# Expert jobs of 128 tokens instead of 256, with the tokens as the stationary operand

## The chip, the cores and the metric

The kernel runs on one core of one Trainium2 chip. The metric is the device time of one execution in microseconds (us). The kernel before was timed three times: 1541.42, 1542.98 and 1551.13 us, a median of 1542.98 us. One further execution was recorded by the hardware profiler; every row below comes from it.

## The reference, cut to what matters

The program computes one layer over 625 nodes of 768 features: a graph attention block, a linear attention block ("mixer"), and a feed-forward block of a shared expert and eight routed experts. The change touches only the routed experts:

```python
h1 = jnp.einsum('td,eid->tei', x2, w1)      # 768 -> 512, each expert e
h3 = jnp.einsum('td,eid->tei', x2, w3)
h = jax.nn.silu(h1) * h3
y = jnp.einsum('tei,edi,te->td', h, w2, cw) # 512 -> 768, weighted by the gate
z = jax.nn.silu(x2 @ sw1.T) * (x2 @ sw3.T) @ sw2.T   # the shared expert
return (y + z)
```

The gate gives every token two experts, so `cw` has 1250 entries that are not zero. The reference's own gate, evaluated on the drawn inputs, sends 332, 144, 157, 53, 209, 113, 224 and 18 tokens to experts 0 to 7.

## The kernel before, in words

The routed part works only on the pairs of token and expert that exist. On the chip, VectorE counts the tokens of each expert, cuts them into **jobs** of `CAP` = 256 places (`BL` = 2 blocks of 128), and writes a list (`lst`) with the token, the target row and the gate weight of each place. The counts above make 2+1+1+1+1+1+1+1 = 9 jobs. A job loads the three weight matrices of its expert whole, in six pieces of 128x1536 float32 (768 KB each): pieces 0 and 1 are w1, 2 and 3 are w3, 4 and 5 are w2.

Products are taken in a split form: each operand is a high part and a low part in the float32r format, and `mm3` (lines 1375 to 1379) issues high x high, high x low and low x high. So each operand passes twice through other engines: ScalarE casts the high part (`split_hi`, line 794, for weights; `tokens_hi`, line 825; line 844 for the hidden rows), VectorE subtracts it to get the low part (`split_lo`, L1192; `tokens_lo`, L1335; L1351). There is one buffer for the raw pieces and one for the split ones (`we`), so piece q of the next job is loaded when `split_lo` has read piece q of this one, and is split when TensorE has used it.

All engines run the same loop over jobs, each its own `body(g, parity)`: jobs 0 and 1 are written out, jobs 2 to `JOBS_MIN` in a loop, the rest in a loop whose bodies are guarded by `If(count > g)`. The order on each engine is fixed by its program:

- GpSimd: gathers the 128-row blocks of the next job's tokens from HBM (`gather_tokens`, indirect DMA, L595), then scatters the two result blocks of this job to `y_rows` (L617) when VectorE has weighted them. The scatter of a block waits until the one before it has landed. The gather of the job after stands behind these scatters in GpSimd's program.
- TensorE: the w1 products of the job (weights stationary, 256 token columns moving), the w3 products, and between them the transposes of the next job's tokens (L1623); then the down products of the same job (hidden rows stationary, 384 columns of w2 moving). An up matrix is 4x6 groups of three matmuls, so 144 matmuls for both; the down products are 48 matmuls.
- ScalarE and VectorE: the splits, Silu (L842), the product with the w3 half (L1349), and the weighting of the result by the gate (L1360, 128x384).
- SyncE: issues the loads of the weight pieces (L472), each after the wait for its buffer.

When all results have landed, SyncE reads `y_rows` back and VectorE adds them to the output (L1368). The shared expert runs before the jobs. While it runs, VectorE makes the job list (`places`, L1251 to L1296), with one instruction for each multiple of `CAP` below 625 (L1262).

Of the kernel before, what the change touches and what calls it, by code (L numbers as in the profile page):

```python
# [17 lines left out]
ALU = mybir.AluOpType  # L18
# [30 lines left out]
CAP = 256  # L49
# [13 lines left out]
def build(nc, x, src, dst, W1s, b1s, W1d, b1d, attn1, ln1_w, ln1_b, Wos, bos, Wod, bod, attno, lno_w,  # L63
          lno_b, qkv_wT, qk_bcols, v_brow, proj_wT, proj_b, proj_matT, gate_wT, gate_bias, moe_w, out):
    ctx = ExitStack()
    with ctx:
# [12 lines left out]
        def dram(name, shape, dt=F32):  # L79
# [66 lines left out]
        jobs_i = sb("jobs_i", [P, 1], I32)  # L146
# [13 lines left out]
        hid_s, raw4, raw5, y_1 = zone([("hid_s", [128, 2, IC, CAP], F32R), ("raw4", [128, PIECE], F32),  # L160
                                       ("raw5", [128, PIECE], F32), ("y_1", [128, D], F32)])
        sb("zone_d", [128, T * N + 4 * D], F32)
        raw3, xg = zone([("raw3", [128, PIECE], F32), ("xg", [128, BL, D], F32)])
# [18 lines left out]

        atg0, atg1, y_0 = zone([("atg0", [128, 2, KC, CAP], F32R), ("atg1", [128, 2, KC, CAP], F32R), ("y_0", [128, D], F32)])
        atg, y_sb = [atg0, atg1], [y_0, y_1]
# [90 lines left out]
        xg_loaded = [sem(f"xg_loaded{i}") for i in range(BL)]  # L275
# [3 lines left out]
        e_hi, e_lo = sem("e_hi"), sem("e_lo")  # L279
# [27 lines left out]
        def jobs(eng, start, body):  # L307

            start()
            for g in range(2):  # L310
                body(g, g)
            with eng.Fori(1, JOBS_MIN // 2) as m:
                for parity in range(2):
                    body(2 * m + parity, parity)
            eng.wait_ge(jobs_ready, 1)
            count = eng.value_load(jobs_i[0:1, 0:1], min_val=JOBS_MIN, max_val=JOBS)
            with eng.Fori(JOBS_MIN // 2, JOBS // 2) as m:
                for parity in range(2):
                    with eng.If(count > 2 * m + parity):
                        body(2 * m + parity, parity)  # L320

        def tg_psum(b):

            return (ps[:, 4 + 2 * b:6 + 2 * b, :].rearrange("p a b -> p (a b)")[:, 1024 - D:1024]
                    .rearrange("p (k n) -> p k n", k=KC))

# [34 lines left out]
        def _(sp):  # L361
# [122 lines left out]
            for q in range(6):  # L484
# [4 lines left out]
                if q >= 4:  # L489
                    sp.wait_ge(e_lo, q - 3)  # L490
                load_piece(ROUTED, q, q % 4)

            def load_pieces(g, qs):
# [3 lines left out]
                for q in qs:  # L497
                    if not isinstance(g, int):
                        sp.wait_ge(e_lo, 6 * g + q + 1)
                    elif q < 4:  # L500
                        sp.wait_ge(e_lo, (5, 6, 3, 4)[q])
                    load_piece(e, q, q)

# [3 lines left out]
            load_pieces(0, (4, 5))  # L507
            with sp.Fori(1, JOBS_MIN) as g:
                load_pieces(g, range(6))
            count = sp.value_load(jobs_i[0:1, 0:1], min_val=JOBS_MIN, max_val=JOBS)  # L510
            with sp.Fori(JOBS_MIN, JOBS) as g:
                with sp.If(count > g):
                    load_pieces(g, range(6))
            load_pieces(count, range(4))

            sp.wait_ge(landed, 16 * BL * count)
# [12 lines left out]
        def _(pool):  # L529
# [59 lines left out]
            def gather_tokens(g):  # L589
                blocks = slice(BL * g, BL * g + BL) if isinstance(g, int) else bass.ds(BL * g, BL)  # L590
                pool.tensor_copy(gather_i[:, :], lst[:, blocks, 0]).then_inc(gather_i_ready, 1)
                pool.wait_ge(gather_i_ready, g + 1)
                for b in range(BL):
                    pool.sem_inc(pool_turn, 1)
                    pool.indirect_dma_start(  # L595
                        out=xg[:, b, :], out_offset=None, in_=xf_rows,
                        in_offset=bass.IndirectOffsetOnAxis(ap=gather_i[:, b:b + 1], axis=0)).then_inc(xg_loaded[b], 16)
# [6 lines left out]
            def body(g, parity):  # L604
                pool.wait_ge(tg_full, BL * g + BL)
                gather_tokens(g + 1)

                if not first(g):
                    pool.wait_ge(landed, 16 * BL * g)
                pool.tensor_copy(scatter_i[:, :], lst[:, bass.ds(BL * g, BL), 1]).then_inc(scatter_i_ready, 1)  # L610
                pool.wait_ge(scatter_i_ready, g + 1)
                for b in range(BL):
                    pool.wait_ge(down_used, 4 * g + 10 + 2 * b + 2)
                    if b > 0:
# [1134 lines left out]
```

## Time and profile before

| | |
|---|---|
| profiled execution, its own time | 1550.59 us |
| span of its core | 1548.8 us |
| median of the three timed runs | 1542.98 us |
| TensorE busy, share of the span | 1108.7 us, 72% |
| VectorE / ScalarE / GpSimd busy | 60% / 35% / 38% |
| bytes moved by DMA | 270.51 MB, 175 GB/s over the span |
| scatters of result blocks (L617) | 18, so 9 jobs of two blocks |
| weight pieces loaded (768 KB each) | 64: 6 for the shared expert, 54 for nine jobs, 4 for a tenth that isn't run |

The two stages of graph attention take most of the span; the job stage lies between 1250 and 1518 us, and from 1518 us on the kernel only reads results back, adds and stores. An engine's busy time is the sum over its instructions; matmuls are pipelined, so the time from one matmul to the next is read from their starts and not from their durations. Times of rows are microseconds from the start of the span.

### The profile page before, as it was taken

To read this page: it belongs to the slowest core of one execution; us is meant where nothing else is said; L and a number is where in the kernel's file an instruction comes from. 1 tells how busy PE (TensorE), PEld (TensorE's weight loads), DVE (VectorE), ACT (ScalarE), POOL (GpSimd) and SP (SyncE) were. 2 spreads that over 40 slices of the span, in tenths; PEclk is the share of its full clock that TensorE was granted. 3 is DMA by queue.
4 is the path that set the end of the run, shared out by engine and by line. 5 is a ranking of instruction groups with operands and counts; after the bars stand their busy time and mean duration, and the time that the engine had idled before them with its cause. 6 is when DMAs were issued, how large, how long until landed. Compare 5 with 4: busy or idle time off the path is not lost.

```text
span 1548.8 us, 17191 instructions
## 1 busy us (share of the span) xinstructions
PE 1108.7 (72%) x6361; PEld 956.7 (62%) x6361; DVE 932.1 (60%) x1695; ACT 536.9 (35%) x754; POOL 586.0 (38%) x578
## 2 busy tenths in 40 slices
PE   6956555555416657998999996008869999989992
PEld 5943333333316647986787775008549999889981
DVE  6548777777757666525445445453786556556564
ACT  3214333333226556202333443001333234434440
POOL 0037777777720000026777777760000001211210
PEclk9986777777857678996999998557977999999996
DMA  9756676767662231348767768643111356755745
GB/s 342 280 195 195 198 198 196 201 195 201 195 164 65 65 86 62 122 145 275 207 204 216 214 194 260 187 143 91 61 60 52 102 224 216 243 194 187 235 148 169
DMA packets 81361, 270.51 MB, mean 175 GB/s; under 512 B 15619, under 2 KB 37417, under 8 KB 80662
## 3 DMA queue, kind: packets, MB, share of 16 engines
q0 software_dynamic: 35296, 148.26, 32.0%
q1 hardware_dynamic: 42502, 107.11, 22.5%
q10 hardware_dynamic: 3488, 14.16, 2.3%
q8 instruction: 46, 0.75, 0.2%
q14 instruction: 29, 0.23, 0.1%
HBM read 236.29 MB, written 33.19 MB: 174 GB/s over the span
## 4 chain that ended last, share of the span: by engine, by line
POOL 29%; PE 25%; DMA 16%; DVE 15%; issue 12%; ACT 3%; SPq 0%; POOLq 0%; DVEq 0%; ACTq 0%
POOL dense_logits L564 10%; POOL ring_s L553 10%; POOL ring_d L559 8%; PE ps L1377 7%; PE ps L1378 7%; PE ps L1379 7%; DMA ring_d<-table_dst,dst_i 5%; DMA xg<-xf_rows,gather_i 3%; DMA y_rows<-y,scatter_i 3%; DVE mxv L1060 3%; DMA dl_a<-dense_logits 3%; DVE ring_s L973 1%; DVE stats L863 1%; PE ps L1468 1%; DMA y_in<-y_rows 1%
## 5 line engine op out<-in xcount | busy, mean ns | idle before, releaser
L973 DVE TENSOR_TENSOR ring_s<-ring_s,ring_d 128x776 f32<-128x776 f32 (+1 forms) x168 | 162.1, 965 | 268.9 <-DMA ring_d<-table_dst,dst_i 268.8
L553 POOL DMA_INDIRECT ring_s<-table_src,src_i x168 | 169.3, 1008 | 397.3 <-DVE fd_stage L902 336.0
L1433 PE MATMUL ps<-hot_s,hot_d 128*125 128x512 f16 (+1 forms) x840 | 185.9, 388 | 157.6 <-DVE hot_s L980 157.5
L1433 PEld LDWEIGHTS ps<-hot_s,hot_d 128*125 128x125 f16 x840 | 116.6, 180 | 227.0 <-DVE hot_s L980 168.1
L564 POOL DMA_INDIRECT dense_logits<-logits,cell_i x168 | 203.0, 1208 | 51.4 <-issue 50.9
L559 POOL DMA_INDIRECT ring_d<-table_dst,dst_i x168 | 164.3, 978 | 51.2 <-issue 51.2
L674 ACT ACTIVATE hot_d<-iota_h,dst_bias 128x626 f16<-128x626 f16 x84 | 68.5, 816 | 219.7 <-PE ps L1433 219.6
L1377 PE MATMUL ps<-atg,we 128*128 128x256 f32 x432 | 123.5, 286 | 2.2 <-DVE atg L1335 2.2
L1378 PE MATMUL ps<-atg,we 128*128 128x256 f32 x432 | 122.5, 284 | 0.0
L1379 PE MATMUL ps<-atg,we 128*128 128x256 f32 x432 | 122.2, 283 | 0.0
L1377 PE MATMUL ps<-wp,at 128*125 128x384 f32 x300 | 105.6, 352 | 7.0 <-DVE at L886 4.1
L1378 PE MATMUL ps<-wp,at 128*125 128x384 f32 x300 | 104.4, 348 | 0.0
L1379 PE MATMUL ps<-wp,at 128*125 128x384 f32 x300 | 104.3, 348 | 0.0
L1468 PE MATMUL ps<-fs,dpt 125*125 125x96 f32 (+1 forms) x500 | 98.7, 358 | 0.0
L1395 PE MATMUL ps<-ident,b 125*128 125x125 f32 x90 | 19.2, 381 | 108.9 <-DVE b L1038 83.9
L617 POOL DMA_INDIRECT y_rows<-y,scatter_i x18 | 17.7, 982 | 200.3 <-DVE y L1360 160.3
L1192 DVE TENSOR_TENSOR we<-eraw,we 128x1536 fp32r<-128x1536 f32 x35 | 60.5, 1756 | 54.3 <-ACT we L794 54.2
L1468 PEld LDWEIGHTS ps<-fs,dpt 125*125 125x125 f32 x500 | 81.6, 233 | 13.1 <-issue 1.8
L1377 PEld LDWEIGHTS ps<-atg,we 128*128 128x128 f32 x432 | 83.0, 192 | 2.4 <-issue 2.4
L1395 PEld LDWEIGHTS ps<-ident,b 125*128 125x128 f32 x90 | 15.4, 201 | 111.6 <-DVE b L1038 84.0
L1509 PE MATMUL ps<-xt,mix_w 128*128 128x313 f32 (+1 forms) x288 | 81.8, 442 | 2.0 <-issue 1.7
L1378 PEld LDWEIGHTS ps<-atg,we 128*128 128x128 f32 x432 | 82.8, 192 | 0.0
(241 smaller groups left out, 2595.5 us busy)
## 6 DMA issues: line engine op xcount, KB each, us to landing
eraw<-in_moe_w_dram SPq DMA_DIRECT2D x35, 768.0 KB, 6.4
raw<-in_moe_w_dram SPq DMA_DIRECT2D x29, 768.0 KB, 6.1
dense_logits<-neg ACTq DMA_DIRECT2D x1, 12288.0 KB, 40.9
mix_w<-in_qkv_wT_dram SPq DMA_DIRECT2D x18, 384.0 KB, 6.5
dl_a<-dense_logits SPq DMA_DIRECT2D x3, 2187.5 KB
dl_b<-dense_logits SPq DMA_DIRECT2D x2, 2187.5 KB
y_in<-y_rows SPq DMA_DIRECT2D x5, 672.0 KB
ring_s<-table_src,src_i POOLq DMA_INDIRECT x168, 4.1
```

The lines of the kernel that those rows point to most:

```text
L553: pool.indirect_dma_start(out=ring_s[:, j, 0:WL[l]], out_offset=None, in_=table_src[l], in_offset=bass.IndirectOffsetOnAxis(ap=src_i[:, t: ...
L559: pool.indirect_dma_start(out=ring_d[:, j, 0:WL[l]], out_offset=None, in_=table_dst[l], in_offset=bass.IndirectOffsetOnAxis(ap=dst_i[:, t: ...
L564: pool.indirect_dma_start(out=dense_logits[l], out_offset=bass.IndirectOffsetOnAxis(ap=cell_i[:, t:t + 1], axis=0), in_=logits[:, t, 0:HL[ ...
L674: act.activation(hot_d[:, j, :], iota_h[:, :], ACT.Square, scale=0.25, bias=dst_bias[:, t:t + 1]).then_inc(hot_square, 1)
L973: dve.tensor_tensor(ring_s[:, j, 0:WL[l]], ring_s[:, j, 0:WL[l]], ring_d[:, j, 0:WL[l]], ALU.add).then_inc(z_ready[l], 1)
L1192: dve.tensor_tensor(we[:, 2 * m + 1, part], src, we[:, 2 * m, part].bitcast(F32), ALU.subtract).then_inc(e_lo, 1)
L1377: pe.matmul(o, lt(0), r(0), start=start, stop=False)
L1378: pe.matmul(o, lt(0), r(1), start=False, stop=False)
L1379: return pe.matmul(o, lt(1), r(0), start=False, stop=stop)
L1433: last = pe.matmul(ps[0:P, b, o:o + s1 - s0], hot_d[:, j, c * P:(c + 1) * P], hot_s[:, j, s0:s1], start=start and (n <= 5 or n == 9), stop ...
L1468: last = pe.matmul(o, pt[:, m * N + s * P:m * N + (s + 1) * P], fs[:, s, col:col + w], start=s == 0, stop=s == T - 1)
L1509: last = pe.matmul(ps[:, b, 0:c1 - c0], mix_w[:, 1 - m, k, s * 128:(s + 1) * 128], xt_v[:, k, c0:c1], start=k == 0, stop=k == KC - 1)
```

## The change

`CAP` becomes 128 and `BL` 1. A job is one block of tokens, with one gather and one scatter. The counts above make 3+2+2+1+2+1+2+1 = 14 jobs. `JOBS_MIN` becomes 10 (it was 4) and `JOBS` 18 (it was 12).

In the up products the operands trade places: the tokens are stationary and 512 columns of a weight matrix move, so a matrix is 6 groups of three matmuls, 36 matmuls for both, and the result has tokens on the partitions. ScalarE and VectorE make Silu and the product in one instruction each of 128x512 (`hid_rows`). The hidden rows then have to be transposed for the down products: four transposes on TensorE into bank 4 (`transpose_hidden`), and a split of 128x512 on ScalarE and VectorE (`hidden_hi`, `hidden_lo`).

The down products of job g-1 (24 matmuls of 384 columns) are issued in body g, behind the up products of job g and the transposes of the tokens of job g+1; the weighting and the scatter of job g-1 move with them. A new `finish` issues the last job's. SyncE loads pieces 0 to 3 of job g+1 ahead of pieces 4 and 5 of job g. The semaphores of the pieces are parted into those for w1 and w3 and those for w2.

```diff
-CAP = 256
+CAP = 128
...
+            finish(eng.value_load(jobs_i[0:1, 1:2], min_val=JOBS_MIN - 1, max_val=JOBS - 1))
...
+            def load_job(g):
+                load_pieces(g + 1, range(4))
+                load_pieces(g, (4, 5))
```

On GpSimd:

```diff
+            def scatter_rows(g):
+                if not first(g):
+                    pool.wait_ge(landed, 16 * g)
+                pool.tensor_copy(scatter_i[:, :], lst[:, bass.ds(g, 1), 1]).then_inc(scatter_i_ready, 1)
+                pool.wait_ge(scatter_i_ready, g + 1)
+                pool.wait_ge(down_used, 2 * g + 12)
...
+            def body(g):
+                pool.wait_ge(tg_full, g + 1)
                 gather_tokens(g + 1)
                 if not first(g):
...
+                    scatter_rows(g - 1)
```

On ScalarE:

```diff
+            def tokens_hi(g):
+                act.wait_ge(tg_full, g + 1)
+                act.copy(atg[:, 0, :, :], tg_psum()).then_inc(tg_hi, 1)
+
+            def hidden_hi(g):
+                act.wait_ge(ht_full, g + 1)
+                act.wait_ge(down_full, 2 * g + 10)
+                act.copy(hid_t[:, 0, :, :], ps[:, HT_BANK, :].rearrange("p (j n) -> p j n", j=IC)).then_inc(hid_hi, 1)
...
+            def body(g):
+                if not first(g):
+                    hidden_hi(g - 1)
                 act.wait_ge(w1_used, g + 1)
                 split_hi(g + 1, (0, 1))
...
+                act.wait_ge(up_full, g + IC + 1)
+                act.wait_ge(hid_f, g + IC)
+                act.activation(silu[:, 0, 0:INTER], ps[:, 0, :], ACT.Silu).then_inc(silu_done, 1)
+                tokens_hi(g + 1)
                 split_hi(g + 1, (2, 3))
...
+                act.wait_ge(down_full, 2 * g + 10)
+                split_hi(g, (4, 5))
```

On VectorE:

```diff
+            def hidden_lo(g):
+                dve.wait_ge(hid_hi, g + IC + 1)
+                dve.tensor_tensor(hid_t[:, 1, :, :], ps[:, HT_BANK, :].rearrange("p (j n) -> p j n", j=IC),
+                                  hid_t[:, 0, :, :].bitcast(F32), ALU.subtract).then_inc(hid_lo, 1)
+
+            def weighted(g):
+                if not first(g):
+                    dve.wait_ge(landed, 16 * g)
+                w = lst[:, bass.ds(g, 1), 2].bitcast(F32)
+                for h in range(2):
+                    dve.wait_ge(down_full, 2 * g + h + 11)
+                    dve.tensor_scalar(y_sb[:, h * HALF:(h + 1) * HALF], ps[:, DOWN_BANKS[h], 0:HALF], w, None, ALU.mult).then_inc(down_used, 1)
...
+            def body(g):
+                if not first(g):
+                    hidden_lo(g - 1)
+                split_lo(g + 1, (0, 1))
+                dve.wait_ge(silu_done, g + IC + 1)
+                if not first(g):
+                    dve.wait_ge(ht_full, g)
+                dve.tensor_tensor(hid_rows[:, :], silu[:, 0, 0:INTER], ps[:, 1, :], ALU.mult).then_inc(hid_f, 1)
+                tokens_lo(g + 1)
+                split_lo(g + 1, (2, 3))
+                if not first(g):
+                    weighted(g - 1)
                 split_lo(g, (4, 5))
```

On TensorE:

```diff
             def transpose_tokens(g):
...
+                pe.wait_ge(xg_loaded, 16 * g + 16)
+                if not first(g):
+                    pe.wait_ge(tg_lo, g)
+                for k in range(KC):
+                    last = pe.transpose(tg_psum()[:, k, :], xg[:, k * 128:(k + 1) * 128], ident[:, :])
+                last.then_inc(tg_full, 1)
+
+            def up(m):
+                for k in range(KC):
+                    last = mm3(ps[:, m, :], lambda s: atg[:, s, k, :], lambda s: w13[m][s][:, k, :], k == 0, k == KC - 1)
+                return last
+
+            def transpose_hidden(g):
+                pe.wait_ge(hid_f, g + IC + 1)
+                for j in range(IC):
+                    last = pe.transpose(ps[:, HT_BANK, j * 128:(j + 1) * 128], hid_rows[:, j * 128:(j + 1) * 128], ident[:, :])
+                last.then_inc(ht_full, 1)
+
+            def down(g):
+                pe.wait_ge(w2_lo, 2 * g + 4)
+                pe.wait_ge(hid_lo, g + IC + 1)
+                pe.wait_ge(down_used, 2 * g + 10)
+                for h in range(2):
+                    for k in range(IC):
+                        last = mm3(ps[:, DOWN_BANKS[h], 0:HALF], lambda s: hid_t[:, s, k, :],
+                                   lambda s: w2v[s][:, k, h * HALF:(h + 1) * HALF], k == 0, k == IC - 1)
+                    last.then_inc(down_full, 1)
...
+            def body(g):
+                pe.wait_ge(up_lo, 4 * g + 6)
+                pe.wait_ge(tg_lo, g + 1)
+                pe.wait_ge(hid_f, g + IC)
+                up(0).then_inc(w1_used, 1)
+                if not first(g):
+                    transpose_hidden(g - 1)
+                pe.wait_ge(up_lo, 4 * g + 8)
+                up(1).then_inc(up_full, 1)
+                transpose_tokens(g + 1)
+                if not first(g):
+                    down(g - 1)
+
+            def finish(last):
+                transpose_hidden(last)
+                down(last)
```

## Rows read from the trace of the kernel before

**Rows 1.** Windows over the job stage; busy us (instructions) of each engine, granted clock, DMA share, GB/s.

```profile
1250.00:1518.00 268.00, 249.02 (x1848) 245.06 (x1848) 158.94 (x181) 117.43 (x146) 41.74 (x52) 0.98 0.61 209
```

**Rows 2.** DMA queues in the job stage: packets, MB, share of 16 engines' time.

```profile
q1 hardware_dynamic: 7776, 42.47, 46.9%
q0 software_dynamic: 2720, 13.37, 13.8%
```

**Rows 3.** Waits of the job stage: who waited for what, us in total, times, longest.

```profile
PE ps L1623 <- DMA xg<-xf_rows,gather_i: 16.7, 12, 3.8
```

**Rows 4.** Timeline of TensorE and chain of waits: starts of the first and last of a run.

```profile
1253.94 0.28 PE L1379 MATMUL ps<-atg,we 128*128 128x256 f32 x1
...
1262.48 0.28 PE L1379 MATMUL ps<-atg,we 128*128 128x256 f32 x1
...
1454.86 0.17 PE ps L1377
...
1458.84 0.19 PE ps L1379
```

**Rows 5.** Groups of instructions, shapes apart, from 1000 us: busy, mean ns, idle before.

```profile
L1192 DVE TENSOR_TENSOR we<-eraw,we 128x1536 fp32r<-128x1536 f32 x35 | 60.5, 1756 | 54.3 <-ACT we L794 54.2
L794 ACT CAST we<-eraw 128x1536 fp32r<-128x1536 f32 x35 | 50.4, 1476 | 49.4 <-PE ps L1379 49.4
L1360 DVE TENSOR_SCALAR y<-ps,lst 128x384 f32<-128x384 f32 x36 | 19.9, 610 | 6.8 <-PE ps L1379 6.8
L1335 DVE TENSOR_TENSOR atg<-ps,atg 128x768 fp32r<-128x768 f32 x20 | 18.6, 955 | 10.8 <-ACT atg L825 10.8
L825 ACT CAST atg<-ps 128x768 fp32r<-128x768 f32 x20 | 15.3, 798 | 22.0 <-PE ps L1623 22.0
L1349 DVE TENSOR_TENSOR silu<-silu,ps 128x256 f32<-128x256 f32 x36 | 15.0, 417 | 12.7 <-ACT silu L842 12.6
```

**Rows 6.** Chain of waits: the weighting of a block and its scatter.

```profile
1459.73 0.62 DVE y L1360
...
1461.16 4.94 DMA y_rows<-y,scatter_i
```

**Rows 7.** Timeline of GpSimd: a scatter and the next gather.

```profile
1317.32 0.98 POOL L617 DMA_INDIRECT y_rows<-y,scatter_i  x1 [4.39 <-DMA y_rows<-y,scatter_i]
...
1319.32 1.00 POOL L595 DMA_INDIRECT xg<-xf_rows,gather_i  x1 [0.82 <-POOL gather_i L591]
```

**Rows 8.** The tile xg (gathers), then first, longest and last of six on the chain.

```profile
DMA to landing us min/median/max: 3.9/5.7/9.6
...
1290.32 6.07 DMA xg<-xf_rows,gather_i
...
1349.69 8.47 DMA xg<-xf_rows,gather_i
...
1470.22 6.15 DMA xg<-xf_rows,gather_i
```

**Rows 9.** Chain of waits: token transposes and the first up product of job 0.

```profile
1249.90 0.89 PE ps L1623 x6
...
1253.62 0.36 PE ps L1377
```

**Rows 10.** Chain of waits: the last scatter.

```profile
1522.48 3.03 DMA y_rows<-y,scatter_i
```

**Rows 11.** Window in which only weight pieces move; columns as in the first group.

```profile
1262.00:1272.00 10.00, 10.00 (x88) 10.00 (x86) 6.82 (x9) 5.92 (x9) 0.00 (x0) 1.00 1.02 422
```

**Rows 12.** Windows around a gap of TensorE, and over the edge stage; columns as before.

```profile
1386.00:1388.00 2.00, 0.00 (x0) 0.00 (x0) 1.53 (x4) 0.69 (x2) 0.45 (x1) 1.00 0.85 304
1388.90:1392.20 3.30, 3.30 (x17) 3.07 (x16) 1.87 (x3) 1.60 (x2) 0.00 (x0) 0.50 0.76 283
...
296.00:500.00 204.00, 99.12 (x500) 70.62 (x500) 147.44 (x224) 76.01 (x96) 109.67 (x105) 0.71 0.62 170
```

**Rows 13.** One line of VectorE: the count of jobs.

```profile
L1262 DVE SCALAR_TENSOR_TENSOR job_count<-before,job_count x2: 168/168/169, 1204.1 to 1204.3; 125x8 f32<-125x8 f32 x2
```

More of the change, by code:

```diff
@@ L274, in build @@
         gather_i_ready, scatter_i_ready = sem("gather_i_ready"), sem("scatter_i_ready")
[L275 removed]
+        xg_loaded, ht_full = sem("xg_loaded"), sem("ht_full")
         tg_full, tg_hi, tg_lo, w1_used = sem("tg_full"), sem("tg_hi"), sem("tg_lo"), sem("w1_used")
@@ L497, in load_pieces @@
                 for q in qs:
[L498 to L501, printed above, removed]
+                    if q >= 4:
+                        if not first(g):
+                            sp.wait_ge(w2_lo, 2 * g + q - 3)
+                    elif not first(g):
+                        sp.wait_ge(up_lo, 4 * g + q + 1)
+                    elif q < 2:
+                        sp.wait_ge(w2_lo, q + 1)
+                    else:
+                        sp.wait_ge(up_lo, q + 1)
                     load_piece(e, q, q)
+            def load_job(g):
+                load_pieces(g + 1, range(4))
+                load_pieces(g, (4, 5))
             sp.wait_ge(jobs_ready, 1)
@@ L512, in _ @@
                 with sp.If(count > g):
-                    load_pieces(g, range(6))
-            load_pieces(count, range(4))
-            sp.wait_ge(landed, 16 * BL * count)
+                    load_job(g)
+            sp.wait_ge(landed, 16 * count)
             for t in range(T):
@@ L602, in start @@
                 gather_tokens(0)
-            def body(g, parity):
-                pool.wait_ge(tg_full, BL * g + BL)
+            def body(g):
+                pool.wait_ge(tg_full, g + 1)
                 gather_tokens(g + 1)
                 if not first(g):
[L609 to L614, printed above, removed]
-                        pool.wait_ge(landed, 16 * BL * g + 16 * b)
-                    pool.sem_inc(pool_turn, 1)
-                    pool.indirect_dma_start(
-                        out=y_rows, out_offset=bass.IndirectOffsetOnAxis(ap=scatter_i[:, b:b + 1], axis=0),
-                        in_=y_sb[b][:, :], in_offset=None).then_inc(landed, 16)
-            jobs(pool, start, body)
+                    scatter_rows(g - 1)
+            def finish(last):
+                scatter_rows(last)
+            jobs(pool, start, body, finish)
         @block.scalar
@@ L1352, in body @@
                 split_lo(g + 1, (2, 3))
                 if not first(g):
-                    dve.wait_ge(landed, 16 * BL * g)
-                for u in range(4):
-                    b, h = u // 2, u % 2
-                    w = lst[:, bass.ds(BL * g + b, 1), 2].bitcast(F32)
-                    dve.wait_ge(down_full, 4 * g + 10 + u + 1)
-                    dve.tensor_scalar(y_sb[b][:, h * HALF:(h + 1) * HALF], ps[:, 4 + u, 0:HALF], w, None, ALU.mult).then_inc(down_used, 1)
-            jobs(dve, start, body)
+                    weighted(g - 1)
@@ L1365, in _, with finish @@
+                split_lo(g, (4, 5))
+            def finish(last):
+                hidden_lo(last)
+                weighted(last)
+            jobs(dve, start, body, finish)
             for t in range(T):
@@ L1619, in transpose_tokens @@
             def transpose_tokens(g):
-                for b in range(BL):
-                    pe.wait_ge(xg_loaded[b], 16 * g + 16)
-                    for k in range(KC):
-                        last = pe.transpose(tg_psum(b)[:, k, :], xg[:, b, k * 128:(k + 1) * 128], ident[:, :])
-                    last.then_inc(tg_full, 1)
+                pe.wait_ge(xg_loaded, 16 * g + 16)
[22 more added lines that the diff above has]
+                    last.then_inc(down_full, 1)
             def start():
```

137 lines of the change are left out of this document (46 added, 91 removed).

## The prediction

> **What bounds the kernel now.** I read the windows first, to find the stage that the change touches: 1250 to 1518 us, 268 us for nine jobs, 29.8 us a job. TensorE is busy 93% of it at a granted clock of 0.98, and the DMA engines 61% [rows 1]. The waits show what ends its idle time: 12 waits for gathered tokens, 16.7 us, where the longest is 3.8 us [rows 3]. So TensorE bounds the stage, with a gather late in most jobs. A busy sum does not price its work; starts do. The 72 steps between the two up matmuls of the timeline take 8.54 us, 0.1186 us for 256 columns, and the 23 steps between the two down matmuls 3.98 us, 0.173 us for 384 [rows 4]. A job before is then 144 x 0.1186 + 48 x 0.173 + 12 transposes (2 x 0.89 [rows 9]) = 17.1 + 8.3 + 1.8 = 27.2 us.
>
> **TensorE after.** 128 columns more cost 0.173 - 0.1186 = 0.055 us, so 512 columns cost 0.228 us; the bounds are 0.213 (512 columns at 2.4 GHz) and 0.237 (twice the 256). Up: 36 x 0.228 = 8.2 us. Down: 24 x 0.173 = 4.15 us. Six token and four hidden transposes at 0.89/6: 1.5 us at most, 1.3 in a stream. Sum 13.7 us (13.1 to 14.1), half of before. But there are 14 jobs instead of 9, and what a job costs the other engines does not halve, since every job splits and loads its expert whole.
>
> **VectorE** after, a job: six subtractions at 1.72 us (a pair takes 3.43, a lone one 1.756 [rows 5]) 10.3; tokens 0.955; weighting two halves 1.1 to 1.2; two new 128x512 instructions, between 0.417 (128x256) and 0.955 (128x768) [rows 5], on the line between them 0.68, so 1.4. Sum 13.8 us. **ScalarE**: 6 x 1.43 to 1.476 + 0.80 + 2 x 0.60 = 10.7 us. It hides beside VectorE.
>
> **DMA.** A job loads 6 x 786 KB = 4.72 MB, as before, and moves one gather and one scatter of 0.393 MB. With only weights moving the engines gave 422 GB/s at a share of 1.02 [rows 11]: 11.2 us for 4.72 MB. Over the whole stage their packets took 46.9% of 268 us for nine sets, 14.0 us a set, and 13.8% for 34 indirect transfers (13.37 MB / 0.393), 1.09 us each [rows 2]. A job after needs between 11.2 + 2.2 = 13.4 and 14.0 + 2.2 = 16.2 us of the DMA engines. The order of the loads costs nothing of its own: a buffer is freed by its subtraction and cast again a period less some 4 us later, and that time covers issue and landing as long as the engines stay under their 16.2; SyncE reads the job's expert twice instead of once, beside its waits.
>
> **The chain that I expect to bound.** Four resources want 13.7 to 16.2 us; a chain through all of them wants more. In body g GpSimd issues gather g+1 and then scatter g-1, which waits for the weighting of job g-1. The gather of the following job stands behind that wait. Follow it once round, from the end of a job's weighting: to the issue of the scatter 1461.16 - 1460.35 = 0.81 us [rows 6]; from that to the issue of the gather 1319.32 - 1317.32 = 2.00 [rows 7]; landing L; six transposes till ScalarE can read 0.92, from the 0.89 of the row [rows 9]; high part of the tokens 0.80; the third piece's high part 1.43; 0.09 to VectorE, whose token subtraction (0.955) fits beside it; two subtractions 3.43; the next weighting 1.10 (the down products, 4.15 us from the end of the transposes, are done by then). That is 10.6 us + L. The tokens' landing has a median of 5.7 us and a range of 3.9 to 9.6; but a gather that comes behind another indirect transfer, as each does after the change, lands later: six such stand on the chain, first 6.07, last 6.15, longest 8.47, median 6.1 and mean 6.6 [rows 8]. I take L = 6.4, so a **period of 17.0 us**; 14.5 with 3.9, where VectorE and the DMA engines would bound instead (15 to 16), and 20.2 with 9.6. TensorE idles 3.3 us of each period, waiting in front of the token transposes.
>
> By the Trainium skill ("DMA: Bandwidth & Descriptors", Anatomy of one DMA), an indirect transfer takes about 2.0 us plus its bytes over 436 GB/s, which is 2.9 us for 0.393 MB. By it the chain would close in 13.5 us, and the sum would go by the DMA engines' bound. The trace does not agree: no gather landed in under 3.9 us.
>
> **The stage in order.** Start: the first token block of a job 0 has six transposes, one cast, one subtraction; before, 3.72 us from the first transpose to the first product [rows 9] with two blocks, now about 2.9, so job 0 starts at 1252.8. It runs without down products: 8.2 + 0.3 + 0.92 + 0.80 + 0.96 = 11.0 us, to 1263.8. Job 1 needs no scatter before its gather; its body is the resources' 13.5 us, to 1277.3. Then eleven periods of 17.0: job 13 starts at 1464.3. Its tail: up products 8.2 and the hidden transposes 0.5, the gap 3.3, token transposes 0.7 and the down products of job 12 4.2 (17.0); ScalarE splits w2 of job 13 in 2.9, VectorE ends 1.9 later, splits the hidden rows 0.8, down products 4.4, weighting of the second half 0.6, 0.8 to the scatter, and 3.0 to land with quiet queues [rows 10]: 31.4 us in all, and I add 1.3 for the guarded bodies 14 to 17 that each engine skips, which no row prices. The last result lands at 1497.0. Before it landed at 1522.48 + 3.03 = 1525.5 [rows 10]. That is 28.5 us less; each us of the period is worth 11. Read-back, adding and storing follow unchanged.
>
> **What else changes.** The dispatch gains two instructions like L1262 and one like it for the last job's number, 3 x 0.17 = 0.5 us [rows 13], and loses a little on a shorter list; I charge 0.5. The drain loses one scatter that waited for another (counted above). The five more weight sets lie in the period. The ends: nothing to 1 us.
>
> **Sum:** 28.5 - 0.5 = 28 us less than the profiled execution's 1550.6, so 1522.6 in that execution's terms. It was 7.6 us above the median of the runs, mostly not in this stage, so against the median: 1543 - 28 = **1515 us**.
>
> **Rivals.**
> (a) **TensorE's clock falls, and it is slower.** Now there is a gap every job. After the gap of 1386 to 1388 us, 2.3 us long, the clock was 0.50 from 1388.9 to 1392.2, and in the edge stage, where TensorE is busy 99 of 204 us, it averages 0.71 [rows 12]. One such fall of 3.3 us costs 1.7 us of TensorE's work; that fits in the gap, and in the chain the down products have 0.5 us to spare, so it costs about 1 us. The rival: the fall lasts. TensorE's 13.7 us at a mean of 0.68 is 20.2 us, plus the waits that remain, a period of 21: 11 x 4 = 44 us more than the forecast, 1559 us. It decides from a period of 19.5, a mean clock below 0.73. Against it: busy 13.7 of 17 us is far more than in the edge stage, and a lower clock closes the gap that lowered it. Chance 0.10.
> (b) **The gather grows late under load, and nothing is gained.** The DMA share would rise from 0.61 to over 0.9. With L = 8.5, as the longest on the chain, the period is 19.1 and the time 1515 + 23 = 1538; with 9.6, 1550. Range of this case 1528 to 1558. For it: 16.2 of 17.0 us is nearly full. Against it: gathers land now while the queues are as full, since pieces are loaded just then. Chance 0.25. The skill's same page (Queues, rings and completion order) says that a DMA engine serves its queue rows in turn, so that a gather would not stand behind the weights' backlog; it would cap L, and speaks for the forecast.
> (c) **The gather is fast, and VectorE or the DMA engines bound.** Period 15.3, 1515 - 19 = 1496. It is also where the page's formula would lead. Chance 0.10.
> (d) **The number of jobs is not 14.** The trace allows 10 to 17 with nine jobs of 256; each is worth a period. The counts are clear of the multiples of 128 by 15 or more, so under 0.01.
> The forecast keeps 0.55.
>
> **Numbers.** The forecast's own range, L from 5.7 to 7.4, is 1507 to 1526. The range for 8 times in 10 takes in (b) up to a period of 20.0 and some of (c): 1499 to 1547. This measurement can tell 1%, 15 us, from no change: faster means below 1527.6, a period under 18.1. Faster: the forecast 0.54, (c) 0.10 and a small part of (b), 0.02: 0.66. Same, to 1558.4: most of (b) and the mildest of (a), 0.23. Slower: 0.11.
>
> **What would show it.** Right: 14 scatters; 17 us between up products of successive jobs; TensorE's largest wait the gather, about 3 us in each job, in front of L1623's transposes; GpSimd's scatter waiting for VectorE and never for landing; up matmuls 0.228 us apart. The clock: above 0.9 by the forecast, below 0.73 by (a). The DMA share: 0.9 or more by (b), with gathers of 8 us. By (c) TensorE waits for VectorE's subtractions instead. Wrong would be a period above 19.5, a wait of ScalarE for raw pieces that I price at nothing, or an interaction at the guarded bodies, jobs 10 to 13.

## The result, and where the time went

The changed kernel takes **1568.9 us** (median of 4 runs, 1561.3 to 1580.5) against 1542.8 us (4 runs) of the kernel before: a ratio of 1.016, 95% interval 1.010 to 1.022. It is slower by 26 us; 1515 us, faster, was predicted. The profiled execution of the changed kernel took 1580.45 us and that of before 1550.59. It was the longest of its four, with the lowest mean clock (0.81, against 0.82 to 0.83), so the turns read below may be a little longer than those of the median run. Of the 29.9 us between the two profiles, 7.3 lie ahead of the job stage, where little but the job list differs (the stage's start lies between 1242.8 and 1257.2 us in the profiles of this study). The stage itself, from the first token transpose to the landing of the last scatter, took 1556.0 - 1257.15 = 298.9 us. Before it took 275.6, and 247.1 was predicted.

Windows of the changed kernel, columns as in [rows 1] (busy us and instructions of PE, PEld, DVE, ACT, POOL; granted clock, DMA share, GB/s): first eleven turns of the loop, from the issue of one gather to the issue of the eleventh after it; then a wait of TensorE, and what follows it; then the end of the stage.

```profile
1298.96:1523.75 224.79, 173.76 (x759) 152.39 (x760) 145.28 (x118) 110.95 (x97) 48.11 (x45) 0.83 0.74 265
...
1405.90:1408.04 2.14, 0.00 (x1) 0.01 (x1) 0.00 (x0) 0.00 (x0) 0.00 (x0) 0.54 1.01 408
1408.04:1412.80 4.76, 4.76 (x17) 4.76 (x18) 1.94 (x2) 3.19 (x3) 0.00 (x0) 0.50 0.49 203
...
1545.00:1551.50 6.50, 6.35 (x24) 6.07 (x24) 0.62 (x1) 0.00 (x0) 0.00 (x0) 0.66 0.00 0
```

Eleven periods in 224.79 us are **20.44 us each**, where 17.0 was predicted. No engine is full: TensorE is busy 77%, VectorE 65%, and the DMA share is 0.74. TensorE is idle 51.0 us, 4.6 a period. The waits of the stage say for what, and answer to [rows 3].

```profile
POOL y_rows L615 <- DVE y_sb L1367: 148.5, 12, 17.4
...
PE ps L1652 <- DMA xg<-xf_rows,gather_i: 57.6, 12, 9.6
```

So TensorE waits for the gather, in every period, and GpSimd for VectorE's weighting: this is the chain that the prediction named. The tile xg, which answers to [rows 8]:

```profile
DMA to landing us min/median/max: 3.8/7.3/9.0
```

One turn of the chain of waits, in order of time (start, us, what):

```profile
1400.57 7.42 DMA xg<-xf_rows,gather_i
...
1408.04 1.55 PE ps L1652 x6
...
1409.61 0.04 ACT atg L836
...
1410.31 1.48 ACT we L806
...
1411.82 0.05 DVE we L1212
...
1415.69 0.62 DVE y_sb L1367
...
1417.12 0.22 POOL y_rows L615
...
1419.57 0.85 POOL gather_i L601
...
1421.20 7.45 DMA xg<-xf_rows,gather_i
```

The timelines of VectorE and of GpSimd over its end answer to [rows 7] (TENSOR_TENSOR of 128x1536 is a subtraction, `split_lo`):

```profile
1413.49 1.75 DVE L1212 TENSOR_TENSOR we<-raw,we 128x1536 fp32r<-128x1536 f32 x1
1415.16 1.14 DVE L1367 TENSOR_SCALAR y_sb<-ps,lst 128x384 f32<-128x384 f32 x2
1416.94 3.43 DVE L1212 TENSOR_TENSOR we<-raw,we 128x1536 fp32r<-128x1536 f32 x2 [0.64 <-ACT we L806]
```

```profile
1417.12 2.45 POOL L615 DMA_INDIRECT y_rows<-y_sb,scatter_i  x1 [11.60 <-DVE y_sb L1367]
1419.57 0.84 POOL L601 COPY gather_i<-lst 128x1 int32 x1
1421.20 1.00 POOL L604 DMA_INDIRECT xg<-xf_rows,gather_i  x1 [0.79 <-POOL gather_i L601]
```

Here the scatter's issue takes 2.45 us and the index copy 0.84; in [rows 7] they took 0.98, and 1.02 with what lies between copy and gather (4.08 us from issue to issue now, 2.00 before). VectorE's pair of subtractions began 0.18 us ahead of the scatter's issue, and the copy ends at 1420.41, just when the pair does (1420.37). Over all 14 jobs the scatter's issue has a mean of 2257 ns, against 982 for the 18 of before (the page's groups):

```profile
L615 POOL DMA_INDIRECT y_rows<-y_sb,scatter_i x14 | 31.6, 2257 | 168.3 <-DVE y_sb L1367 168.3
```

The turn of 20.63 us, beside the prediction's 16.98:

| step | predicted | 1400.57 to 1421.20 | difference |
|---|---|---|---|
| gather to TensorE's start | 6.40 | 7.47 | +1.07 |
| six transposes until ScalarE reads | 0.92 | 1.57 | +0.65 |
| tokens' high part, third piece's cast, handover | 2.32 | 2.21 | -0.11 |
| two subtractions | 3.43 | 3.34 | -0.09 |
| weighting | 1.10 | 1.15 | +0.05 |
| weighting to the scatter's issue | 0.81 | 0.81 | 0 |
| scatter's issue to the next gather's | 2.00 | 4.08 | +2.08 |

Over the eleven turns the step from the scatter's issue to the gather's has a mean of 3.89 us (2.63 to 4.21), the way from the gather's issue to TensorE's start 7.46, and the transposes 1.58; the other steps keep their time within 0.02 us. Three terms carry the miss: GpSimd's two instructions, the landing, and the transposes at the lower clock. The experiments act on each.

### The profile page after: what moved, and what is told of

It is laid out like the page before. It is cut to its first block, busy times and chain, and to the rows that moved or that the text cites. A ratio compares the mean times of both kernels' runs of the same rounds, so it can differ in the third digit from the quotient of the medians.

```text
span 1578.7 us, 15823 instructions
## 1 busy us (share of the span) xinstructions
PE 1079.6 (68%) x5499; PEld 903.6 (57%) x5499; DVE 963.3 (61%) x1671; ACT 564.7 (36%) x735; POOL 612.4 (39%) x579
## 4 chain that ended last, share of the span: by engine, by line
POOL 29%; PE 18%; DMA 18%; DVE 15%; issue 15%; ACT 3%; SPq 2%; DVEq 0%; POOLq 0%; ACTq 0%
POOL dense_logits L574 10%; POOL ring_s L563 10%; POOL ring_d L569 8%; DMA ring_d<-table_dst,dst_i 6%; DMA xg<-xf_rows,gather_i 6%; PE ps L1405 5%; PE ps L1406 5%; PE ps L1407 5%; DVE mxv L1077 3%; DMA dl_a<-dense_logits 3%; DMA wraw<-in_W1d_dram 2%; DVE ring_s L990 1%; PE ps L1652 1%; PE ps L1496 1%; DVE we L1212 1%
## 5 line engine op out<-in xcount | busy, mean ns | idle before, releaser
L574 POOL DMA_INDIRECT dense_logits<-logits,cell_i x168 | 211.7, 1260 | 51.4 <-issue 50.9
L1212 DVE TENSOR_TENSOR we<-eraw,we 128x1536 fp32r<-128x1536 f32 x50 | 86.4, 1755 | 22.9 <-ACT we L806 22.8
L601 POOL COPY gather_i<-lst 128x1 int32 (+1 forms) x15 | 12.9, 860 | 220.1 <-DVE lst L1325 188.2
L615 POOL DMA_INDIRECT y_rows<-y_sb,scatter_i x14 | 31.6, 2257 | 168.3 <-DVE y_sb L1367 168.3
L1031 DVE SCALAR_TENSOR_TENSOR ring_d<-ring_s,rows 128x768 f32<-128x768 f32 x84 | 80.6, 959 | 0.0
L1212 DVE TENSOR_TENSOR we<-raw,we 128x1536 fp32r<-128x1536 f32 x44 | 76.0, 1755 | 7.1 <-ACT we L806 7.1
L1006 DVE TENSOR_REDUCE head_sum<-ring_s 128x8 f32<-128x768 f32 x84 | 80.1, 953 | 0.0
L1002 DVE SCALAR_TENSOR_TENSOR ring_s<-ring_s,rows 128x768 f32<-128x768 f32 x84 | 79.9, 951 | 0.0
```

Of the source, the lines that this page charges most:

```text
L574: pool.indirect_dma_start(out=dense_logits[l], out_offset=bass.IndirectOffsetOnAxis(ap=cell_i[:, t:t + 1], axis=0), in_=logits[:, t, 0:HL[ ...
L1031: dve.scalar_tensor_tensor(out=ring_d[:, j, 0:D], in0=ring_s[:, j, 0:D], scalar=0.0, in1=rows[:, 2, :], op0=ALU.max, op1=ALU.mult, accum_o ...
L1212: dve.tensor_tensor(we[:, 2 * m + 1, part], src, we[:, 2 * m, part].bitcast(F32), ALU.subtract).then_inc(up_lo if q < 4 else w2_lo, 1)
```

## The experiments

A period is the mean of eleven, from gather issue to gather issue inside the loop, the first ones of the stage left out. Ratios are to the kernel before, run on the same chip, which gave 1545.7, 1542.0 and 1542.4 us there.

**VectorE's subtractions kept off GpSimd's issue.** In the changed kernel, VectorE starts pieces 4 and 5 only when GpSimd has issued scatter and gather.

```diff
                 gather_tokens(g + 1)
+                pool.sem_inc(port_free, 1)
                 if not first(g):
...
                     weighted(g - 1)
+                    dve.wait_ge(port_free, g + 2)
                 split_lo(g, (4, 5))
```

> The changed kernel with one wait: VectorE starts the subtractions of pieces 4 and 5 only when GpSimd has issued the next gather; nothing else moves. In the changed kernel the scatter's issue takes 2.4 us and the index copy 0.84 us, and both end about where VectorE's subtractions end. Theory A with the cause in VectorE's subtractions holding GpSimd up: the scatter's issue goes back to 1.0 us and the copy to 0.2, gather issue 2.0 us after the scatter's, the period from 20.5 to 18.5, the time down by about 21 us to 1548. If the DMA queue's load lengthens GpSimd's instructions instead: they stay at 2.4 and 0.84 us, the period stays or grows by up to 1 us, since VectorE now waits about 3 us more.

Measured: 1546.1 us, 0.9999 (0.997 to 1.003). The 22.8 us are what the first theory asked for (21). GpSimd's timeline, and VectorE's pair, now behind the scatter:

```profile
1377.33 0.99 POOL L616 DMA_INDIRECT y_rows<-y_sb,scatter_i  x1 [10.74 <-DVE y_sb L1370]
1378.33 0.20 POOL L602 COPY gather_i<-lst 128x1 int32 x1
1379.31 2.56 POOL L605 DMA_INDIRECT xg<-xf_rows,gather_i  x1 [0.79 <-POOL gather_i L602]
```

```profile
1379.24 3.43 DVE L1215 TENSOR_TENSOR we<-raw,we 128x1536 fp32r<-128x1536 f32 x2 [2.73 <-POOLq L628]
```

The issue that runs beside the pair is the long one: now the gather's takes 2.56 us, and TensorE, which the chain goes to next, waits for the landing alone. (One turn of the changed kernel is an exception: the scatter issued at 1355.35, 0.02 us behind the start of a pair, took 1.00 us; the copy and the gather behind it took 0.84 and 1.70.) From issue to issue it is 1.98 us, as in [rows 7]. The period is 18.45 us; with L = 7.4 the prediction's own sum gives 18.0. The shorter wait of TensorE also brought 0.28 us of the transposes' time back.

**The gap filled.** 36 transposes of the identity into a free bank, ahead of the token transposes.

```diff
                 up(1).then_inc(up_full, 1)
+                for _ in range(FILL):
+                    pe.transpose(ps[:, 7, 0:128], ident[:, :], ident[:, :])
                 transpose_tokens(g + 1)
```

> The changed kernel with 36 idle transposes of the identity (4 us) into an unused PSUM bank between TensorE's w3 products and its wait for the gathered tokens; their result is not used. Theory A: the clock stays at 1.0, the token transposes take 0.88 us instead of 1.55, so the chain shortens by 0.7 us (up to 1.5 if the down products were late), 8 to 16 us in all: 1553 to 1561. Theory C (the low clock is the main cost): the period falls by the 2.3 us of TensorE's work that the low clock adds or more, to 18 or less, 27 us or more: 1542 or less.

Measured: 1562.4 us, 1.011 (1.007 to 1.015), 1.4 us above the range of theory A. It is 6.5 us less than the changed kernel, but the two intervals (1.010 to 1.022 there) overlap, so the times alone do not show a gain. The window after:

```profile
1300.00:1500.00 200.00, 185.56 (x1087) 165.84 (x1088) 136.46 (x112) 106.93 (x93) 42.82 (x40) 0.98 0.76 280
```

The clock is back at 0.98 and the period is 19.54 us, 0.90 less. That is not all the clock's: the transposes give 0.61 of it. The fill also moved GpSimd's issues against VectorE's pairs, so that the step from scatter to gather fell by 0.47 us (the scatter's issue took 1.71 us in most turns), and the gathers landed 0.17 later. The landings of this run say something more. Three gathers had an issue of 2.58 us, beside a pair, and took 8.46 to 8.51 us to land; those with an issue of 1.00 took 7.00 to 7.78. The granted clock costs little here; most of the work that it slows lies beside the chain.

**Less to load.** Pieces 4 and 5 of jobs after the first load 128 of their 1536 columns, and the down products use old weights.

```diff
-                    load_piece(e, q, q)
+                    if q >= 4 and not first(g):
+                        sp.dma_start(raws[q][:, 0:128], moe_w[bass.ds(e, 1), q, :, 0:128]...)
+                    else:
+                        load_piece(e, q, q)
```

> The changed kernel, but pieces 4 and 5 (w2) of all jobs except the first load only 128 of their 1536 columns; the rest of the piece keeps the first job's values, so the down products use old weights. The engines' instructions are the same. It takes away 31% of the weights' bytes. Theory A1: the gather's landing grew from the 5.7 us of the kernel before to 7.3 us because weights crowd it; with fewer bytes it falls to 5.5 to 6, and the period from 20.5 to 18.8 to 19.2, the time by 14 to 20 us, to 1549 to 1555. Theory A2: the landing is set by the queues taking turns, whatever the backlog: the landing stays at 7 us and the time within 6 us of 1569.

Measured: 1532.6 us, 0.993 (0.989 to 0.997), 36 us less than the changed kernel, where at most 20 were expected. The tile xg of this kernel:

```profile
DMA to landing us min/median/max: 3.7/4.6/8.4
```

The period falls from 20.44 to 17.60 us. The median of the landings misleads here, because they come in two kinds, as two neighbours on the chain show:

```profile
1300.01 8.39 DMA xg<-xf_rows,gather_i
...
1320.89 4.10 DMA xg<-xf_rows,gather_i
```

Gathers whose own issue took 1.00 us landed in 3.7 to 4.7 us, where the changed kernel has 6.8 to 7.8. The four whose issue ran beside a pair and took 2.58 us landed in 7.3 to 8.4. Over the eleven turns the way from issue to TensorE's start falls by 1.98 us (7.46 to 5.48), the step through GpSimd by 0.45, and the transposes by 0.43; together they are the 2.84 but for rounding. So most of the gather's lateness comes from the pieces of the same job that move beside it. Of the three edits this one gains the most time, but only two thirds of its gain in the period is the landing.

**Two terms together.** The first edit and 24 filling transposes.

> The changed kernel with two of the suspected terms taken away together: VectorE's subtractions of pieces 4 and 5 wait until GpSimd has issued the next gather, and 24 identity transposes into a free bank fill TensorE's gap before the token transposes. Alone the first gave 1546.1 us and the second (36 transposes) 1562.4 us against 1568.9. Theory A, the terms are separate and add up: 1546 less about 0.6 us of transposes at the low clock in each of 12 jobs, 1536 to 1542 us. Theory B, the first change had already brought the clock back (0.92 between 1300 and 1500 us, 0.83 in the changed kernel) and nothing is left for the second: 1544 to 1552 us.

Measured: 1545.2 us, 1.001 (0.998 to 1.004), within the range of theory B. The fill works, as the granted clock of 1300 to 1480 us shows:

```profile
1300.00:1480.00 180.00, 164.04 (x935) 144.51 (x934) 131.71 (x109) 103.59 (x90) 46.61 (x40) 1.00 0.83 301
```

But its period, 18.29 us, is only 0.16 below that of the first edit alone, whose clock was already 0.92 from 1300 to 1500 us. The turns in parts, means of the same eleven, read from the starts in the timelines:

| step, us | predicted | changed | subtractions later | gap filled | less to load | both terms |
|---|---|---|---|---|---|---|
| gather's issue to TensorE's start | 6.40 | 7.46 | 7.63 | 7.63 | 5.48 | 7.86 |
| transposes until ScalarE reads | 0.92 | 1.58 | 1.30 | 0.97 | 1.15 | 0.91 |
| from there to the weighting | 5.75 | 5.55 | 5.55 | 5.56 | 5.56 | 5.56 |
| weighting and handover to the scatter's issue | 1.91 | 1.96 | 1.98 | 1.96 | 1.96 | 1.96 |
| scatter's issue to the next gather's | 2.00 | 3.89 | 2.00 | 3.42 | 3.44 | 2.00 |
| period | 16.98 | 20.44 | 18.45 | 19.54 | 17.60 | 18.29 |

So the transposes' term did go: 0.28 us with the first edit, 0.39 more with the fill. The gathers of this run landed 0.23 us later, which took over half of that back. Why they did is not shown. The low clock was in good part a consequence of the chain, since a shorter wait of TensorE alone brought the clock from 0.83 to 0.92.

**The gather taken out of the ring.** The changed kernel with the gather issued one job earlier, ahead of the wait for the weighting; job 0's start issues two.

```diff
                 gather_tokens(0)
+                pool.wait_ge(tg_full, 1)
+                gather_tokens(1)
...
             def body(g):
-                pool.wait_ge(tg_full, g + 1)
-                gather_tokens(g + 1)
+                pool.wait_ge(tg_full, g + 2)
+                gather_tokens(g + 2)
```

> The changed kernel with one move: GpSimd issues the gather of job g+2 as soon as the token transposes of job g+1 are done, ahead of the scatter of job g-1, instead of behind it. Theory A (the chain scatter issue, index copy, gather, transposes, subtractions, weighting sets the period of 20.5 us): the chain is cut, TensorE's 120 us of waits for xg go, the period falls to what VectorE (13.8 us), TensorE (14) and the DMA engines (16) need, 15.5 to 16.5 us, and the time falls by about 11 x 4.4 = 48 us to about 1520 us, below the kernel before. Theory B (the DMA engines' volume sets it: five more weight sets, share 0.74): the period stays at 19 to 20.5 us and the time within 12 us of 1569. Theory C (TensorE's low clock sets it): period 18 to 20, since the gap shrinks only in part.

Measured: **1480.5 us** (1477.2 to 1487.8), 0.960 (0.955 to 0.964), the fastest kernel here, 65 us below the 1545.7 of before on the same chip and 40 below the 1520 that was expected. GpSimd's timeline, and the window from 1300 to 1400 us:

```profile
1339.11 0.99 POOL L604 DMA_INDIRECT xg<-xf_rows,gather_i  x1 [0.80 <-POOL gather_i L601]
1340.10 1.53 POOL L611 COPY scatter_i<-lst 128x1 int32 x1
1345.13 1.72 POOL L615 DMA_INDIRECT y_rows<-y_sb,scatter_i  x1 [3.51 <-DVE y_sb L1369]
...
1352.68 1.00 POOL L604 DMA_INDIRECT xg<-xf_rows,gather_i  x1 [0.79 <-POOL gather_i L601]
```

```profile
1300.00:1400.00 100.00, 100.00 (x512) 87.13 (x511) 97.54 (x82) 75.47 (x66) 34.30 (x30) 1.00 1.01 405
```

The landing is little faster (median 6.7 us against 7.3) and the scatter's issue is still long (1.72 us), and neither is waited for. The period is 13.65 us, below the 15.5 to 16.5 that was expected: TensorE's sum of 13.7 was right, and the DMA engines do not need 16.2.

**Which of the full resources sets 13.65 us.** The gather-early kernel with the cut loads.

> The gather-early kernel (1480.5 us), with the loads of weight pieces 4 and 5 cut to 128 of 1536 columns for jobs after the first; the down products use old weights there, so the output is not the reference's. It asks what sets the 13.65 us per job of the gather-early kernel, where both TensorE (100.00 of 100.00 us) and the DMA engines (share 1.01, 405 GB/s) are full. Theory A, TensorE sets it: the pitch of products stays, the period stays within 0.1 us, the time stays at 1477 to 1484 us while the DMA share falls to about 0.73. Theory B, the loads set it and TensorE's records only look full: with 1.4 MB less per job the period falls by up to 1 us, 12 periods, 1466 to 1475 us.

```profile
1300.00:1400.00 100.00, 100.00 (x513) 87.04 (x512) 97.27 (x81) 75.25 (x66) 35.24 (x29) 1.00 0.84 302
```

Measured: 1486.8 us, 0.962 (0.958 to 0.966), 3 us above the range of A. The share falls to 0.84 (0.73 was expected), the GB/s from 405 to 302, and the period stays: 13.61 us, and the stage at 212.9 us against 212.8. (The profiled stage starts 9.6 us later in this run, which is outside of what the edit touches.) So the loads do not set it. TensorE, busy all of the time, is the likely bound; VectorE is at 97%, and no run took work off it.

**The same early gather in the kernel before.**

```diff
-                pool.wait_ge(tg_full, BL * g + BL)
-                gather_tokens(g + 1)
+                pool.wait_ge(tg_full, BL * (g + 1) + BL)
+                gather_tokens(g + 2)
```

> The kernel before with the same move as the first of these runs: the gather of job g+2 is issued when the token transposes of job g+1 are done, ahead of the two scatters. If the kernel before too was held up by gathers that stand behind scatters, TensorE's 16.7 us of waits for xg go and with them the falls of its clock behind them (about 2 us each, three or four): 18 to 25 us less, 1518 to 1525 us. If the waits are only traded for others (the weights' splits), it stays within 5 us of 1543.

Measured: 1524.4 us, 0.987 (0.984 to 0.991), 21 us below before. The stage takes 252.1 us, and TensorE has no gap left:

```profile
1250.00:1490.00 240.00, 239.29 (x1824) 238.29 (x1823) 156.09 (x180) 113.09 (x144) 36.96 (x53) 1.00 0.66 230
```

**The change in its parts, with the gather early in each.** First the small jobs alone: `CAP` 128 in the kernel just shown, weights stationary and 128 token columns moving.

```diff
-CAP = 256
+CAP = 128
```

> The kernel before with the gather moved ahead (1524 us) and CAP = 128 alone: weights stay stationary and 128 token columns move, hidden rows need no transposes, down products stay in their own job. It tells what small jobs are worth without the exchange of operands. If a matmul's time goes by its moving columns (0.065 us for 128): up products 9.4, down 4.2, transposes 0.7 and 1 to 2 us of waits, a period of 15.5 to 16.5, 225 us for 14 jobs against 241 for nine: about 1510 us. If the load of the stationary operand sets a floor near the 0.1186 us of 256 columns: 17.1 + 4.2 + 0.7 and waits, a period of 22 to 23 us, about 1524 + 75 = 1600 us.

Measured: 1594.3 us, 1.032 (1.026 to 1.038), the slowest kernel here and near the 1600 expected of a floor. Matmuls of 128 columns start (1402.93 - 1399.81) / 28 = 0.111 us apart, hardly closer than the 0.1186 of 256 columns in [rows 4]:

```profile
1399.81 0.28 PE L1379 MATMUL ps<-atg,we 128*128 128x128 f32 x1
...
1402.93 0.28 PE L1380 MATMUL ps<-atg,we 128*128 128x128 f32 x1
```

Then the tokens stationary, but the down products of a job in its own body: the gather-early kernel with these orders put back on every engine.

```diff
-                load_pieces(g + 1, range(4))
                 load_pieces(g, (4, 5))
+                load_pieces(g + 1, range(4))
...
-                if not first(g):
-                    scatter_rows(g - 1)
+                scatter_rows(g)
...
-                if not first(g):
-                    down(g - 1)
+                transpose_hidden(g)
+                down(g)
```

> The changed kernel with the gather moved ahead (period 13.65 us, TensorE-bound), and the deferral of the down products undone: hidden transposes, their split and the down products of job g stand in body g, pieces 4 and 5 are split and loaded first in a body, as in the kernel before. Theory: TensorE then waits in each job from the end of the w3 products for Silu 0.6, product 0.7, transposes 0.6, two splits 1.3 and hand-overs, 3.3 to 4 us less the 0.7 of the token transposes, so a period of 16.3 to 17 us, 38 to 47 us more than the kernel with the deferral: 1518 to 1528 us. If the deferral is worth nothing: within 6 us of 1480.

Measured: 1521.3 us, 0.988 (0.984 to 0.991), period 17.1. TensorE now waits inside each job, for the hidden rows and for their split:

```profile
PE ps L1402 <- DVE hid_t L1358: 19.0, 12, 1.6
...
PE ps L1660 <- DVE hid_rows L1378: 15.2, 14, 4.1
```

The stages add up to a ledger: 252.1 us with jobs of 256, 319.6 with small jobs alone, 250.6 with the tokens stationary, 212.8 with the down products one job later. In this order small jobs alone lose 67.5 us, the exchange of operands gives 69.0 back, and the later down products give 37.8; together they are worth 39 us of stage, if the gather is out of the way. In the change as made they lost 23. Neither the exchange nor the later down products were run with jobs of 256, so what they are worth there is not shown.

## Why the prediction was wrong

**Bound and shape: right.** The ring through GpSimd bounds, TensorE waits in front of L1652's transposes in 12 jobs, there are 14 scatters, and the scatter waits for VectorE and never for a landing. The sum of TensorE was right (0.233 us for 512 columns where 0.228 was taken, 13.65 us a job where 13.7 was), and so was the 680 ns of the new 128x512 product.

**The step that failed is the size of the ring, 10.6 us + L.** The eleven periods were 3.46 us longer than the sum on average, and the chain has three terms for it, of 1.89, 1.06 and 0.66 us, less 0.15 in the other steps:

1. *"from that to the issue of the gather 1319.32 - 1317.32 = 2.00"*. It measured 4.08 in the turn shown and 3.89 on average, and with VectorE's pair moved away 1.98 and 2.00 again; that gave 22.8 us of the time back. It was the deciding error. The row was taken where VectorE was quiet. The change puts the subtractions of pieces 4 and 5 directly behind the weighting that releases the scatter, so in the new order the two always meet. The prediction listed what VectorE does, and not what it does at the moment that GpSimd is on the chain. One row of before had the sign of it: the gather of 1349.69, the longest of [rows 8], was issued beside a pair of subtractions that began at 1349.48, and its issue took 2.40 us.

```profile
1349.69 2.40 POOL L595 DMA_INDIRECT xg<-xf_rows,gather_i  x1 [0.30 <-issue]
```

By the Trainium skill ("SBUF — State Buffer", Who interferes with whom) a VectorE instruction with two inputs in SBUF contends with a GpSimd instruction that reads SBUF, over a shared port pair that is an exclusive lock. The index copy agrees: 0.84 us instead of 0.20, ending with the pair. The page infers that a `tensor_tensor` does not hold up descriptor generation; here the issues of scatter and gather beside the pair take 2.45 and 2.56 us instead of 0.99. Whether the reading of the indices or the making of the descriptors is held up, no run here shows.

2. *"I take L = 6.4"*. The median was 7.3, and the mean over the eleven turns 7.42. This is rival (b) in part: a gather beside a job's pieces lands later, and cutting two of six pieces brought the mean to 5.44. The prediction read a cap on L from the turns that the queue rows take (the Trainium skill, "DMA: Bandwidth & Descriptors", Queues, rings and completion order). Whether there is one, no run shows; it did not keep the landing at 6.4, which follows the load in the other queue. The formula's 2.9 us (Anatomy of one DMA) is as far off for gathers as before, since none landed in under 3.7 us in any run, while the last scatter, of the same size and alone in the queues, landed in 3.0. The forecast's L came from gathers of a kernel that moves 209 GB/s, for one that moved 265, and from six of the eight gathers on the chain of before; all eight have a mean of 6.2. This term alone would have left the result within the range.

3. *"so it costs about 1 us"*, of the low clock, said of one fall and charged nowhere. It comes in every period: the clock fell to 0.50 behind the wait of 4.5 us, as in [rows 12], and took 0.66 us a turn in the transposes. The mean of the eleven turns was 0.83, neither above 0.9 nor below the 0.73 from which rival (a) decides, and filling the gap gave 0.61 us a turn of it back. The mechanism of (a), a lasting fall that makes TensorE the bound, did not occur.

Eleven periods make 38 of the 51.8 us by which the stage missed, 247.1 against 298.9; the rest lies at its ends. Job 2's first up product started at 1287.73 and job 13's at 1517.69, 43.0 us more than eleven periods of 17.0. Ten of these intervals have a mean of 20.45 us. The first, ahead of the eleven turns counted above, is 25.42: there the scatter's issue took 3.40 us and the index copy 3.10, both beside VectorE's subtractions, so that 7.30 us passed from the one issue to the other. It is the first error again, at its largest:

```profile
1291.66 3.40 POOL L615 DMA_INDIRECT y_rows<-y_sb,scatter_i  x1 [17.38 <-DVE y_sb L1367]
1295.07 3.10 POOL L601 COPY gather_i<-lst 128x1 int32 x1
```

Job 0 took 14.0 us instead of 11.0, because its first 14 matmuls came some 0.43 us apart after the waits of the start, where 0.233 is the pitch at the full clock. The timeline of TensorE, first job and first of the second:

```profile
1259.96 0.76 PE L1405 MATMUL ps<-we,atg 128*128 128x512 f32 x1 [1.93 <-issue]
...
1265.21 0.63 PE L1405 MATMUL ps<-we,atg 128*128 128x512 f32 x1
...
1273.98 0.47 PE L1405 MATMUL ps<-we,atg 128*128 128x512 f32 x1 [1.93 <-DVE atg L1354]
```

The tail took 38.3 us instead of 32.7; the last down products, at a clock of 0.66 (the last window above), are part of it. 43.0 + 3.0 + 5.6 is 51.6.

**The bounds.** The need of the DMA engines was put between 13.4 and 16.2 us. Only its low end held: with the gather early they moved 5.5 MB in 13.65 us. So the share of time that packets take ([rows 2]) is not a need; bytes over the highest rate seen ([rows 11]) was the better end. Had it been trusted, the range would have been no better, because what missed was the length of the ring.

**The chances.** The case "slower" had 0.11 and one mechanism, the clock. None of the rivals was the one that decided, an instruction on the ring that grows because of its neighbour. The prediction said that each us of the period is worth 11, by which 2.5 us a period lose all 28 us of gain, and still held the ring's steps to a row each, with no bounds except on L.

**What stays open.** The cut loads gave 36 us where the period accounts for 11 x 2.84 = 31. Why the landing depends on the other queue as it does was not taken apart further, nor why gathers with a stretched issue landed late where the fill or the cut loads were in, and little later where the subtractions had been moved. The one scatter that was not stretched beside a pair is not explained.

## What to carry to other kernels

When a loop is bound by a ring of small steps through several engines, price each step in the neighbourhood that it will have after the change, above all what VectorE runs while GpSimd issues, and give each step two bounds; a miss is multiplied by the number of turns. Better still, take the transfer out of the ring: one gather issued a job earlier was worth 88 us here, and 21 in the kernel before. A change that shortens an engine's work should be tried together with the move that keeps that engine fed; alone it can look like a loss.

## What the runs showed of the hardware

- GpSimd's issue of an indirect transfer takes 0.94 to 1.01 us alone, and 1.7 to 2.6 us beside VectorE's subtractions of 128x1536 (3.4 in the first scatter, 1.0 once); a copy of 128x1 takes 0.2 us alone, and 0.5 to 1.8 beside them (3.1 in the longest).
- The gather's landing, counted from the start of its issue: 8.46 to 8.51 us with an issue of 2.58, against 7.00 to 7.78 with one of 1.00, in the kernel with the gap filled; 7.1 to 8.3 in the one with the subtractions later, where the issue took 2.45 to 2.56; 3.7 to 4.7 with an issue of 1.00 and 31% of the weights' bytes away.
- A matmul in float32r with 128 moving columns costs 0.111 us and one with 256 0.119, each with its own weight load; with 384 it is 0.173 and with 512 0.233.
- The DMA engines moved 405 GB/s for 100 us, with indirect transfers among them, while TensorE was busy all of the time.
